# Graph network of four layers: attention and relation layers fetch by group and compute by group-block pair

## The reference

```python
xl = x @ Wl + bl;  xr = x @ Wr + br;  e = edge_attr @ We     # edge_attr: one number per edge
m = jax.nn.leaky_relu(xl[src] + xr[dst] + e, 0.2)
logits = m @ att
# softmax of the logits over the edges of each dst, then the sum of alpha * xl[src]
```

## Time and profile before

| | |
|---|---|
| median of 3 runs | 9534.12 us (9529.4 to 9540.29) |
| span of the profiled execution | 9538.2 us |
| PE busy | 7672.1 us (80%) |
| DVE busy | 7425.2 us (78%) |
| POOL busy | 6583.7 us (69%) |
| ACT busy | 4456.3 us (47%) |

### The profile page before, as it was taken

The page is one execution under the profiler, slowest core; times in us unless marked ns, Lnnn a source line. Parts: engine busy times, 40 slices in busy tenths (PEclk is TensorE's granted clock), DMA queues, the critical chain, the costliest instruction groups (busy, mean ns, idle before and its releaser), DMA issues. The chain is left out here.

```text
span 9538.2 us, 252507 instructions
## 1 busy us (share of the span) xinstructions
PE 7672.1 (80%) x57046; PEld 5545.5 (58%) x57047; DVE 7425.2 (78%) x28322; ACT 4456.3 (47%) x9179; POOL 6583.7 (69%) x6970
## 2 busy tenths in 40 slices
PE   3699999995877777759868888888876888888887
PEld 2344455554655655649856666666654666666665
DVE  6567777776566666669879999999988888888887
ACT  4366666662111111113357777777763444444443
POOL 4777777773777777762237777777765777777775
PEclk7555555558677788789989999999998999999999
DMA  6355555553333444438612222222212222222222
GB/s 176 105 144 145 147 150 150 150 147 90 108 110 111 114 114 117 116 113 268 226 46 68 68 68 67 68 68 68 67 58 56 67 67 67 67 67 67 67 67 66
DMA packets 1175487, 978.10 MB, mean 103 GB/s; under 512 B 745779, under 2 KB 913771, under 8 KB 1175021
## 3 DMA queue, kind: packets, MB, share of 16 engines
q0 software_dynamic: 257328, 554.40, 19.9%
q10 hardware_dynamic: 309758, 261.00, 9.4%
q1 hardware_dynamic: 608320, 161.81, 7.4%
HBM read 688.61 MB, written 245.26 MB: 98 GB/s over the span
## 5 line engine op out<-in xcount | busy, mean ns | idle before, releaser
L1896 POOL DMA_INDIRECT a_far<-node_table,a_rows x1784 | 1683.4, 944 | 706.7 <-issue 542.5
L2132 POOL DMA_INDIRECT r_far<-node_table,r_rows x1784 | 1705.2, 956 | 559.7 <-issue 543.0
L1704 POOL DMA_INDIRECT message_records<-hs,f_pos x1564 | 1516.2, 969 | 623.9 <-issue 424.9
L1298 POOL DMA_INDIRECT near<-split_table,t_rows x1568 | 1516.7, 967 | 492.0 <-issue 476.9
L1775 ACT ACTIVATE f_hot_t<-banks 128x512 bf16<-128x512 bf16 x444 | 265.1, 597 | 1726.5 <-PE banks L1790 1654.4
L1801 PE MATMUL banks<-near,f_hot_t 128*128 x5292 | 528.1, 258 | 477.2 <-DVE hs L1753 471.5
L1491 PE MATMUL banks<-near,t_hot 128*128 x5292 | 693.7, 304 | 175.9 <-SPq L1273 127.7
L1500 PE MATMUL banks<-near,w_f 20*128 20x512 f32 x784 | 809.0, 1133 | 18.9 <-DVE t_positive L1376 18.4
L1491 PEld LDWEIGHTS banks<-near,t_hot 128*128 128x128 bf16 x5292 | 585.5, 135 | 321.4 <-issue 236.7
L1801 PEld LDWEIGHTS banks<-near,f_hot_t 128*128 128x128 bf16 x5292 | 417.8, 115 | 578.5 <-issue 556.7
L2259 PE MATMUL banks<-near,r_hot_t 128*128 x5328 | 672.9, 225 | 32.2 <-DVE r_kind_t L2159 0.2
(11 more groups left out here) (436 smaller groups left out, 19725.6 us busy)
## 6 DMA issues: line engine op xcount, KB each, us to landing
f_soft<-soft_groups ACTq DMA_DIRECT2D x447, 256.0 KB
soft_groups<-near ACTq DMA_DIRECT2D x392, 256.0 KB
m_rows<-message_records SPq DMA_DIRECT2D x223, 264.0 KB
m_rows<-message_records POOLq DMA_DIRECT2D x223, 264.0 KB
acc<-a_cur SPq DMA_DIRECT2D x440, 65.0 KB
acc<-r_cur SPq DMA_DIRECT2D x440, 65.0 KB
a_far<-node_table,a_rows POOLq DMA_INDIRECT x1784
r_far<-node_table,r_rows POOLq DMA_INDIRECT x1784
```

The source lines that it names most:

```text
L1298: pool.indirect_dma_start(far[:, u * KG + q, :], None, k.table3[:, :], bass.IndirectOffsetOnAxis(ap=rows[:, u, q, C_SRC:C_SRC + 1].bitcast ...
L1704: pool.indirect_dma_start(k.mrec[:, :], bass.IndirectOffsetOnAxis(ap=pos[:, u, q:q + 1], axis=0), msg[:, u * KG + q, :], None)\
L1896: pool.indirect_dma_start(far[:, u, q, 0:D], None, k.table[:, :], bass.IndirectOffsetOnAxis(ap=rows[:, u, q, C_SRC:C_SRC + 1].bitcast(I32) ...
L2132: pool.indirect_dma_start(far[:, u, q, 0:D], None, k.table[:, :], bass.IndirectOffsetOnAxis(ap=rows[:, u, q, M_DST - M_SRC:M_DST - M_SRC + ...
```

## The change

The attention and the relation layer now fetch the 392 fixed groups and compute by pair, as `sum_targets` does. POOL's and SP's loops run over groups (`total=NGA, exact=True`), those of DVE, ACT and PE over the 440 pair steps, each reading its group and block from the lists (`pair_group`, `pair_window`). SP announces groups in order (`records_in`, `rows_here`) and frees them (`rows_free`) once all pairs up to a group are summed (`pairs_until`). `cur` is stored by ACT with a copy, not by SP with a DMA. The parts as they stand in `gat_edges`:

```diff
-    LOAD, COLS, KEYS, GATHER, HOT, NEAR, SCORE, MAX, SUM, ADD = 10, 7, 6, 6, 5, 4, 3, 2, 1, 0
+    LOAD, HERE, SENT, FREE = 8, 7, 3, 0
+    COLS, KEYS, HOT, NEAR, SCORE, JOIN, MAX, SUM, ADD = 8, 7, 6, 5, 4, 3, 2, 1, 0
@@ SP
                 def load(g, a):
-                    wait(sp, now, scores, g, a, S)
-                    e0 = first_edge(sp, k, o, g + a)
+                    e0 = moved + (g + a) * GE
                     ...
+                    sp.dma_start(weight[:, u, :], k.wrows[:, bass.ds(e0, GE)]).then_inc(loads_in[u], 16)
-                def keep(g, a): ...
+                def here(g, a):
+                    sp.wait_ge(loads_in[a % S], slot_count(now, g, a, 32, s_load[a % S]))
+                    sp.sem_inc(records_in, 1)
+                def send(g, a):
+                    sp.wait_ge(gathered[a % S], slot_count(now, g, a, 16 * KG, s_gather[a % S]))
+                    sp.sem_inc(rows_here, 1)
+                def free(g, a):
+                    sp.wait_ge(summed, pairs_until(sp, k, o, g + a))
+                    sp.sem_inc(rows_free, 1)
+                skewed(sp, (FREE, free), (LOAD, load), (HERE, here), (SENT, send), counts=now, turn=S, total=NGA, exact=True)
@@ POOL
-                    wait(pool, now, summed, g, a, S)
+                    pool.wait_ge(rows_free, now(g, a + 1))
-                            far[:, u, q, 0:D], None, k.table[:, :],
+                            far[:, u, q, 0:D + 2], None, k.gtable[:, :],
@@ DVE
                 def meet(g, a):
-                    dve.wait_ge(gathered[u], slot_count(now, g, a, 16 * KG, S, s_gather[u]))
+                    group = pair_group(dve, k, o, g + a)
+                    slot = bass.ds(slot_of(group), 1)
+                    dve.wait_ge(rows_here, in_order(group))
+                    nc.vector.scalar_tensor_tensor(line[:, b, :], flat(rows[:, slot, :, C_WT]), even[:, :], flat(far[:, slot, :, D + 1]),
+                                                   ALU.mult, ALU.add)
                     ...
-                    nc.vector.tensor_tensor(met, met, term[:, b, :, :], ALU.add).then_inc(in2, 1)
                 def score_edges(g, a):
-                    nc.vector.tensor_tensor(near_ps[b], near_ps[b], term[:, b, :, :].rearrange("p q d -> p (q d)"), ALU.max)\
+                    (four products: max(value, 0) * 0.8 att, summed on the way, into raw)
+                def join(g, a):       score part 0 = raw + line
+                def rest(g, a):       part 1 = part 0 - its upper half
+                def last_rest(g, a):  part 2 = part 1 - its upper half
-                skewed(dve, (SCORE, meet), (HOT, one_hots), (MAX, node_max), (ADD, add), (COLS, columns), (SCORE, score_edges),
+                skewed(dve, (JOIN, join), (SCORE, meet), (JOIN, rest), (HOT, one_hots), (JOIN, last_rest), (MAX, node_max),
+                       (ADD, add), (COLS, columns), (SCORE, score_edges),
@@ ACT
-                skewed(act, (SUM, take_prob), (MAX, carry), (SCORE, lean), (KEYS, take_keys), (MAX, weigh), (NEAR, terms), ...
+                skewed(act, (SUM, take_prob), (MAX, carry), (KEYS, take_keys), (MAX, weigh), (JOIN, take_parts), (ADD, keep), ...
@@ PE
                 def rows_near(g, a):       (the twelve products, and per q one more:)
+                        last = nc.tensor.matmul(span, flat(weight[:, slot, q:GE:KG]), term[:, :], start=False, stop=True)
+                def turn_parts(g, a):      (one bfloat16 product, 12 columns by 128, onto parts_ps)
                 def spreads(g, a):
+                    wait(pe, now, parts_taken, g, a)
-                        last = nc.tensor.matmul(spread_ps[b][:, q * P:(q + 1) * P], score[:, u, q:q + 1].to_broadcast([P, P]),
-                                                k.ident[:, :], start=False, stop=q == KG - 1, skip_group_check=True)
+                        last = nc.tensor.matmul(spread_ps[b][:, q * P:(q + 1) * P], pick[:, q, :], parts_t[:, b, :],
+                                                start=False, stop=q == KG - 1, skip_group_check=True)
-                skewed(pe, (MAX, spreads), (SUM, sums), (KEYS, spread_keys), (NEAR, rows_near), (MAX, turn_prob), ...
+                skewed(pe, (MAX, spreads), (SUM, sums), (KEYS, spread_keys), (NEAR, rows_near), (JOIN, turn_parts), (MAX, turn_prob), ...
```

More of the change, by code:

```diff
@@ new lines, in _ @@
+                link(nc.vector.tensor_tensor(which[:, :], which[:, :], k.ident[0:16, 2 * KG:3 * KG], ALU.add))
+                for q in range(KG):
+                    nc.vector.tensor_scalar(pick[:, q, :], k.ones_b[0:3 * KG, :], which[0:3 * KG, q:q + 1], None, ALU.mult)
+                split3(nc, link, split[0][:, :], split[1][:, :], split[2][:, :], We[0:9, :], left[:, :])
+                nc.vector.tensor_scalar(att8[:, :], att[:, :], 0.8, None, ALU.mult)
+                nc.vector.scalar_tensor_tensor(work[:, 0, :], We[:, :], 0.2, att[:, :], ALU.mult, ALU.mult, accum_out=even[:, :])
@@ L1927, in meet, with score_edges @@
                     wait(dve, now, near_ready, g, a)
                     met = near_ps[b].rearrange("p (q d) -> p q d", d=D)
[L1929 removed]
+                    nc.vector.tensor_tensor(met, met, far[:, slot, :, 0:D].rearrange("p a q d -> p (a q) d"), ALU.add).then_inc(in1, 1)
+                def score_edges(g, a):
+                    b = a % 2
                     wait(dve, now, in1, g, a)
[L1931 removed]
@@ L1943, in score_edges, with join, rest @@
                     last.then_inc(scores, 1)
+                def join(g, a):
+                    b = a % 2
+                    wait(dve, now, scores, g, a)
+                    wait(dve, now, parts_turned, g, a, 2)
+                    nc.vector.tensor_tensor(score[:, b, 0, :], raw[:, b, :], line[:, b, :], ALU.add).then_inc(joined, 1)
+                def rest(g, a):
+                    b = a % 2
+                    wait(dve, now, joined, g, a)
+                    nc.vector.tensor_tensor(score[:, b, 1, :], score[:, b, 0, :], high(score[:, b, 0, :]), ALU.subtract).then_inc(rested, 1)
@@ L1945, in node_max, with last_rest @@
+                def last_rest(g, a):
+                    b = a % 2
+                    wait(dve, now, rested, g, a)
+                    nc.vector.tensor_tensor(score[:, b, 2, :], score[:, b, 1, :], high(score[:, b, 1, :]), ALU.subtract).then_inc(parted, 1)
                 def node_max(g, a):
@@ L2135, in gather @@
                             .then_inc(gathered[u], 16)
-                skewed(pool, (GATHER, gather), counts=now, turn=S)
+                skewed(pool, (SENT, gather), counts=now, turn=S, total=NGA, exact=True)
             @block.vector
```

550 lines of the change are left out of this document (320 added, 230 removed).

## The result

The changed kernel takes **11287.6 us** (median of 4 runs, 11277.7 to 11302.0), the kernel before 9533.7 us in the same sitting: ratio **1.184**, 95% interval 1.182 to 1.186. The forecast was 10470 us, with a range up to 10950. The direction and the loop were right; the clock inside the loop, the work of a free step and a stop in DVE's queue were not.

A forecast was written before the change was run, and what follows sets the result against it. The prediction took POOL's gathers to bound both layers, with DVE next. From the profiled 9538 us, attention +929, relation -22 and the rest +24 gave 10469 by the profiled span, forecast as 10470 us; range 9900 to 10950.

The forecast's parts named there:

- the loop: Attention: SP's wait for sums ahead of its announcement closes a chain over SP, DVE, ACT, PE; 7.4 us a step.
- free step: Attention: a step whose chain is slack because a group among the three behind has two pairs; 146 of 440, 4.65 us.
- tight ones: Attention: steps in which the loop binds; 294 of 440, forecast at 8.3 us each.
- The clock: Attention: PE's waits lower its clock, so a tight step takes 8.3 us, between 7.4 and 9.6; layer +929 us.
- the filter's share: Clock mix taken from the filter layer: about 57% of the time at 2.4 GHz, the rest at 1.2.
- The rival of 10950 us: Attention: the loop closes and the clock stays low, as longer steps thin PE's work; total 10950 us, chance 0.13.
- Attention, work per step: Attention with all data there: DVE 4.65 us, PE 4.6, ACT under 4; about 4.65 us where nothing else binds.
- the loop never closes: First rival, attention: DVE and PE bind at 4.65 us a step; total 9396 us, chance 0.13.
- Relation: -22 forecast: Relation: the loop doesn't bind, DVE does, at 4.99 us a step against 5.04; -22 us.
- The bound I had set (+70): Relation's upper bound: both value loads bare at 0.2 us more, and the addresses; +70 us.
- The rest: Outside the two layers' steps: packing 12 us, `fresh_rows` 12, other parts 0; +24 us.

The follow-up runs named there:

- e1: Changed kernel, but in attention SP announces group i+5 instead of i+3 in its turn i: 10356.5 us, ratio 1.085 to the kernel before.
- e2: Changed kernel, but in attention SP issues its two loads after the announcement instead of before it: 10913.0 us.
- e15: e13 with SP's announcement in attention put back to group i+3, as in the changed kernel: 10695.2 us.
- e3: Changed kernel plus 24 filling 128x128 products on TensorE per attention step, ahead of its wait for the exponentials: 11006.1 us.
- e10: e1 plus e9, with DVE's loop in attention also turning every 4 steps instead of 8: 10111.3 us, ratio 1.061 to the kernel before.
- e11: e10 with attention's four weight products per step grouped behind the twelve node-row products: 9633.0 us, ratio 1.010 to the kernel before.
- e9: Changed kernel, but in relation DVE's loop turns every 4 steps instead of 8, with one added copy per step: 11137.4 us.
- e12: e11 with the group numbers loaded earlier in DVE's queue in both layers: 9384.8 us, ratio 0.984 to the kernel before.
- e13: e12 corrected so only the first of twelve node-row products carries the start flag: 9400.0 us, ratio 0.983 to the kernel before.

## Why the prediction was right and wrong

**The loop** was right. Its path is the one in the traces, 7.52 us at the upper level (forecast 7.4) and 9.48 at the lower (9.6), and DVE's longest wait is `meet`'s on SP's announcement. Its parts fit too: in the turn shown above, SP takes 1.5 us from the end of the sums (6013.2) to the announcement (forecast 1.55, though the items listed for it add up to 1.45), and `spreads` holds the sums up by 0.9 us (0.8). e1, e2 and e15 show the loop. 285 steps took over 9 us where I counted 294 tight ones.

**The step that failed is "The clock".** It took the filter's share, 57% of the time at 2.4 GHz, and so 8.3 us for a tight step. The granted clock was 0.60 to 0.68 in this layer, and PE's parts of the loop ran at the lower level. On the 294 steps that makes 294 x (9.5 - 8.3) = 353 us. Of the total's miss of 818 us this is the largest single part; without it the time would have been 10935 us, within my range. The error in kind: I took a clock from a stage whose pace POOL sets, and laid it on one in which PE's own waits are part of the loop. There slow products lengthen the wait, and the longer wait keeps the clock down, as e3 and e15 show from either side. The rival of 10950 us named this and had 0.13; the row that spoke for it was that nothing outside the loop sets its pace.

**"Attention, work per step" was mis-sized**, and with it the free steps, 4.65 us. With 294 steps at 9.5, 3731 us leave 6.42 us for each of the other 146: 1.77 x 146 = 259 us. PE takes 5.8 us at the upper clock, not 4.6: the 16 products of different height take 2.1 us, not 1.1 (e10, e11). DVE takes 5.07 us (the shortest frequent step of e1, and most steps of e11), not 4.65: its two value loads cost 1.4 us of idle time (0.79 and 0.58 on average in e11), where I had 0.9. The rest is the lower clock, and the stop at DVE's turn, partly hidden behind the waits here.

So the first rival, "the loop never closes", was priced wrong too. It gave 9396 us; with the loop open the kernel takes 10356 (e1).

**Relation: -22 forecast, +210 measured.** That the loop doesn't bind there was right; its ordinary steps are 4.9 to 5.5 us, 5.12 on average in e9, against a forecast of 4.99. What the sum did not hold is the stop of 2.9 us at each of 54 turns: e9 removes 173 us of the layer's time with the body's length. The bound I had set (+70) counted operations and loads only; a cost of the longer loop body itself was a term put at nothing, without a reason. The value load in `columns` is bare for 0.7 us, not 0.44. Moved, it gives 0.4 us a step (5.11 in e11, 4.69 in e12).

**The rest**: +24 forecast; +42.5 came ahead of attention's first `add` and -40.0 between the layers and behind them. Of the 42.5, some 21 are attention's longer start (from its first gather to its first `add`: 25.5 us before, 46.9 after). The 40 I had not looked at, though the numbers were at hand: 446 groups gathered and 440 used is the 24 gathers too many for which everything waits at a layer's end. 35 of the 40 us are this wait. That this term came near zero is luck: two misses of opposite sign.

The sum against the profiled span: attention +612, relation +232, the rest -22, together the 822 us between 10469 and 11290.9.

## What to carry to other kernels

When an engine that serves several purposes waits for the end of a pipeline (a slot's release) ahead of telling the start of it something that it already knows, the two become one loop. Write down, for every wait in a queue, which step it needs and what stands behind it; here two steps more of lead in one line were worth 931 us in the changed kernel and 1295 in the mended one. A loop that contains the engine whose clock falls when it waits is to be priced at the lower clock first; here the step that ran most often was 9.5 us, not 7.5 or a mean of the two. And "fewer of what bounds" is worth only as much as the next engine leaves: with POOL relieved and every fault found mended, PE holds attention at 5.0 us a step.

## What the hardware showed that I had not expected

- A loop body of 319 or 403 instructions on DVE stops its queue for some 3 us at each backward branch, one of 296 does not (0.23 us), PE's of 828 neither (0.31 us). The bytes of the instruction queue go with it, 4.90, 2.68 and 0.45 MB with two, one and no long body. The Trainium skill (Runtime: NRT & Kernel Launch, Instruction fetch mechanics) says that a taken branch whose target lies outside the two blocks held forces a fetch, and gives most engines room for 512 instructions and PE for 2048. The traces agree on the kind of stop and on PE being spared; on DVE it already appears at 319, well under 512. No run here shows how the blocks lie, nor where between 296 and 319 the stop sets in.
- Products with a 9-row stationary block between products of 128 rows cost about 0.14 us per change: 2.09 us for sixteen mixed, 1.25 for the same sixteen grouped with six changes fewer. Whether it is the height or the change of operands that costs was not separated.
- The start flag of one product reset what other quarters of the same bank had gathered, which showed as soon as the quarters' sums were interleaved (e11, e12) and was gone with a single flag (e13). The Trainium skill (PSUM — Partial Sum Buffer, The four PSUM rules) says just that: the first product's flag clears the marks of the whole 2 KiB bank, and products without it overwrite where a mark is clear.
- The clock can be bought: 24 useless products a step brought it from 0.62 to 0.92 and the kernel 281 us forward, and 8 of them from 0.83 to 1.00 and 126 us forward. Taking away the causes of PE's waits did more.
